# Self-attention's queries and keys projected with features on partitions, two tiles of tokens at a time

## What is computed

```python
x = x + xattn(layernorm(x), ctx_768, mask, Wq, Wk, Wv, Wo)
# self-attention, 16 heads of 32 features
y = layernorm(x)
q = (y @ wq).reshape(b, s, 16, 32)
k = (y @ wk).reshape(b, s, 16, 32)
v = (y @ wv).reshape(b, s, 16, 32)
q, k = rope(q), rope(k)      # out[2i] = t[2i]*cos - t[2i+1]*sin
                             # out[2i+1] = t[2i]*sin + t[2i+1]*cos
p = softmax(where(causal, q @ k.T / sqrt(32), -inf))
x = x + (p @ v) @ wo
x = x + ffn(layernorm(x), ...)
```

## Time and profile before

| | us |
|---|---|
| median of 3 runs (1341.51 to 1342.31) | 1341.54 |
| the profiled execution | 1341.61 |
| its span, first to last instruction | 1339.8 |
| PE busy in the span | 1326.3 |
| POOL busy, 284 instructions | 545.6 |

### The profile page before, as it was taken

The page is one execution under the profiler, slowest core; times in us unless marked ns, Lnnn a source line. Parts: engine busy times, 40 slices in busy tenths (PEclk is TensorE's granted clock), DMA queues, the critical chain, the costliest instruction groups (busy, mean ns, idle before and its releaser), DMA issues.

```text
span 1339.8 us, 33391 instructions
## 1 busy us (share of the span) xinstructions
PE 1326.3 (99%) x13124; PEld 1049.8 (78%) x13124; DVE 689.2 (51%) x1693; ACT 728.6 (54%) x1412; POOL 545.6 (41%) x284
## 2 busy tenths in 40 slices
PE   7999999999999999999999999999999999999998
PEld 6877777777777777777777777778888888888786
DVE  4254544545445444545445444446666578755623
ACT  6455656656566656656566565665343355634231
POOL 6722422432342233224224323654434444473562
PEclk9999999999999999999999999999999999999999
DMA  7101010010001111111100103010000002333241
GB/s 261 60 27 34 29 57 26 33 55 29 33 33 51 33 33 51 33 33 29 55 31 28 59 25 127 14 57 2 2 1 0 0 2 65 95 94 95 79 141 63
DMA packets 39333, 66.20 MB, mean 49 GB/s; under 512 B 4208, under 2 KB 8560, under 8 KB 39280
## 3 DMA queue, kind: packets, MB, share of 16 engines
q1 hardware_dynamic: 38848, 64.67, 14.8%
q10 hardware_dynamic: 432, 0.79, 0.2%
HBM read 61.25 MB, written 4.19 MB: 49 GB/s over the span
## 4 chain that ended last, share of the span: by engine, by line
PE 96%; DVE 1%; POOL 1%; ACT 1%; issue 0%; DMA 0%; POOLq 0%; DVEq 0%
PE psum L205 41%; PE psum L990 9%; PE psum L253 8%; PE psum L1972 7%; PE psum L1596 7%; PE psum L223 5%; PE psum L241 5%; PE psum L1014 3%; PE psum L262 3%; PE psum L775 2%; PE psum L1032 1%; PE psum L1024 1%; PE psum L1042 1%; PE psum L1571 1%; PE psum L1079 0%; PE psum L1074 0%
## 5 line engine op out<-in xcount | busy, mean ns | idle before, releaser
L303 ACT ACTIVATE PT<-psum 128x512 f32<-128x512 f32 x256 | 153.2, 598 | 225.2 <-PE psum L253 225.2
L290 ACT ACTIVATE prob<-prob,nmx 128x512 f32<-128x512 f32 x256 | 182.6, 714 | 96.5 <-DVE nmx L349 96.5
L363 DVE COPY V<-psum 128x512 f32<-128x512 f32 x128 | 88.6, 692 | 228.1 <-PE psum L205 228.1
L349 DVE CUSTOM_DVE_ANT_0 prob<-psum,mbias 128x512 f32<-128x512 f32 x256 | 165.4, 684 | 67.1 <-PE psum L223 67.1
L296 ACT ACTIVATE prob<-prob,rinv 128x512 f32<-128x512 f32 x256 | 182.7, 714 | 0.0
L496 POOL TENSOR_SCALAR ctx_a<-ctx_r 128x1536 fp32r<-128x1536 f32 x16 | 65.4, 4090 | 279.9 <-PE psum L205 279.7
L496 POOL TENSOR_SCALAR ctx_b<-ctx_r 128x1536 fp32r<-128x1536 f32 x16 | 65.4, 4091 | 235.4 <-PE psum L205 235.4
L253 PEld LDWEIGHTS psum<-ident,prob 128*128 128x128 f32 x1024 | 127.6, 141 | 33.4
L253 PE MATMUL psum<-ident,prob 128*128 128x128 f32 x1024 | 153.1, 272 | 0.0
L205 PE MATMUL psum<-wv_h,ctx_b 128*128 128x512 f32 x384 | 144.4, 417 | 0.0
L205 PE MATMUL psum<-wv_h,ctx_a 128*128 128x512 f32 x384 | 142.1, 412 | 0.0
(11 more groups left out here) (236 smaller groups left out, 2810.3 us busy)
## 6 DMA issues: line engine op xcount, KB each, us to landing
ctx_r<-in_ctx SPq DMA_DIRECT2D x32, 768.0 KB, 4.6
w_r<-in_L_ffn_W SPq DMA_DIRECT2D x64, 256.0 KB, 2.8
xres<-in_x SPq DMA_DIRECT2D x16, 256.0 KB, 2.6
out<-tok SPq DMA_DIRECT2D x13, 256.0 KB, 3.0
tok<-in_x SPq DMA_DIRECT2D x3, 1024.0 KB, 11.9
mask<-in_mask_BxS_bf SPq DMA_DIRECT2D x32, 64.0 KB, 4.1
tok<-in_x SPq DMA_DIRECT2D x4, 256.0 KB, 3.4
wq_r<-in_L_xattn_Wq SPq DMA_DIRECT2D x4, 256.0 KB, 5.1
```

What stands on the lines that cost most here:

```text
L290: act.activation(prob[:, r, :], prob[:, r, :], ACT.Exp, bias=nmx[:, r:r + 1], scale=-1.0, accum_out=rsum[:, r:r + 1]).then_inc(s_ex, 1)
L303: act.activation(PT[:, r, :, :].rearrange("p k n -> p (k n)"), T_bank, ACT.Copy).then_inc(s_Pt, 1)
L349: dve.tensor_tensor_reduce(prob[:, r, :], S_bank[r], mbias[:, b, :], 1.0, 3.0e38, ALU.add, ALU.min, nmx[:, r:r + 1]).then_inc(s_mx, 1)
L363: dve.tensor_copy(item_place(q, m), KV_bank[m % 2]).then_inc(s_KVe, 1)
```

## The change

Queries and keys are now computed transposed: the weights are the stationary operand (128 of their columns), and the tokens of a pair of tiles stream past them (256 columns), so the result has features on partitions and needs no transposes. One unit is q or k of one pair: 48 matmuls of 128x256, in four blocks of 12; an even step makes the queries of the pair t+2, t+3, an odd step the keys of that pair. Blocks 0 and 1 go into bank 2, 2 and 3 into bank 3, and each bank is rotated by itself. A rotation is now a product with the cosines and a shuffle of partitions on DVE, a product with the sines and a sum on POOL (`pool_rotate`). ACT's copies of q and k are gone. The tokens of tile t+4 are transposed in step t (before t+2), which takes a second pair of buffers. The loop has four steps in its body. At the end of the cross-attention PE now makes queries and keys of pair 0 and transposes the tokens of tiles 1 to 3, and `v_bank` is gone: values always go into bank 1 behind `s3_od` (tile 15's into bank 3).

```diff
+        def project_pair(pe, b, pair, w_h, w_l, blocks):
+            y_h, y_l = x3_h[pair], x3_l[pair]
+            for j in blocks:
+                out = b[:, j % 2 * 2 * P:(j % 2 + 1) * 2 * P].rearrange("p (t n) -> p t n", t=2)
+                for k in range(DT):
+                    for i, (w, y) in enumerate(((w_h, y_h), (w_l, y_h), (w_h, y_l))):
+                        ins = pe.matmul(out, w[:, k, j * P:(j + 1) * P], y[:, :, k, :], ...)
...
         # pe3
+            if units(t):
+                pe.wait_ge(s3_xl, min(t + 4, G) if isinstance(t, int) else t + 4)
+                pe.wait_ge(s3_rq, 2 * t + 4)
+                at_least(pe, s3_x, t - 2)
+                project_pair(pe, bank[2], pair, w_h, w_l, (0, 1)).then_inc(s3_Q, 1)
+                pe.wait_ge(s3_rk, 2 * t + 4)
+                project_pair(pe, bank[3], pair, w_h, w_l, (2,))
...
-                for n in range(DT):
-                    ins = pe.transpose(bank[0][:, n * P:(n + 1) * P], q_r[:, n * P:(n + 1) * P], ident[:])
...
+            if has(t + 4):
+                pe.wait_ge(s3_rk, 2 * t + 6)
+                pe_x(pe, t + 4, bank[3])
             if has(t + 1) and not (isinstance(t, int) and t == G - 2):
...
+                at_least(pe, s3_od, t)
+                pe.wait_ge(s3_v, t + 1)
+                project_values(pe, bank[1], ph + 1).then_inc(s3_V, 1)
...
+        def rotate(dve, place, rotated):
+            dve.tensor_tensor(by_position(r_cos[:]), by_position(place),
+                              rope[:, 0:1, :].broadcast_to([P, UNIT, SQ]), ALU.mult).then_inc(rotated, 1)
+            dve.stream_shuffle(r_sin[:], place, SWAP).then_inc(rotated, 1)
+        def rotate_low(dve, t):
+            dve.wait_ge(s3_Q, t + 3)
+            at_least(dve, s3_ak, t + 2)
+            rotate(dve, bank[2], s3_rq)
+        def rotate_high(dve, t):
+            dve.wait_ge(s3_K, t + 3)
+            dve.wait_ge(s3_aq, t + 3)
+            rotate(dve, bank[3], s3_rk)
+        def pool_rotate(pool, t, ph, h, rotated, done):
+            x = (k_T if ph % 2 else q_T)[1 - ph // 2]
+            pool.wait_ge(rotated, 2 * t + 6)
+            pool.tensor_tensor(by_position(r_sin[:]), by_position(r_sin[:]),
+                               rope[:, 1:2, :].broadcast_to([P, UNIT, SQ]), ALU.mult).then_inc(s3_am, 1)
+            pool.wait_ge(s3_am, 2 * t + 5 + h)
+            at_least(pool, s3_S, t)
+            pool.tensor_tensor(x[:, 2 * h:2 * h + 2]..., r_cos[:], r_sin[:], ALU.add).then_inc(done, 1)
```

More of the change, by code:

```diff
@@ L900, in dve_cross @@
             END = G - 1, GPT - 1
+            dve_x(dve, 1, 1, bank[2])
             for r in range(3):
@@ L992, in project, with project_values @@
             return ins
[L994 to L1000, removed]
-            return ins
+        def project_pair(pe, b, pair, w_h, w_l, blocks):
[4 more added lines that the diff above has]
+                    for i, (w, y) in enumerate(((w_h, y_h), (w_l, y_h), (w_h, y_l))):
+                        ins = pe.matmul(out, w[:, k, j * P:(j + 1) * P], y[:, :, k, :], start=(k == 0 and i == 0),
+                                        stop=(k == DT - 1 and i == PRODUCTS - 1))
+            return ins
+        def project_values(pe, b, ph):
+            pair, e = ph // 2 % 2, ph % 2
+            return project(pe, b, x3_h[pair][:, e], x3_l[pair][:, e], vw_h, vw_l)
         def pe_x(pe, t, place):
@@ L1016, in output_projection, with scores @@
             return ins
-        def scores(pe):
+        def scores(pe, ph):
+            pair, e = ph // 2 % 2, ph % 2
             for n in range(DT):
@@ L1188, in act3 @@
                 act_normalize(act, 1, (2, 3))
-            if has(t + 2):
-                act_x(act, t + 2, par, x_bank(t + 2))
+            if has(t + 4):
+                act_x(act, t + 4, ph, bank[3])
             if has(t):
@@ L1306, in dve3 @@
                 dve.tensor_tensor(one_tile(t - 2), bank[2], one_tile(t - 2), ALU.add).then_inc(s3_x, 1)
-            if has(t + 2):
-                dve_x(dve, t + 2, par, x_bank(t + 2))
+            if has(t + 4):
+                dve_x(dve, t + 4, ph, bank[3])
             if isinstance(t, int) and t == G - 3:
@@ L1351, in steps @@
             for t in range(4):
-                step(eng, t, t % 2)
-            with eng.Fori(2, G // 2 - 2) as h:
-                for i in range(2):
-                    step(eng, 2 * h + i, i)
+                step(eng, t, t)
+            with eng.Fori(1, G // 4 - 1) as h:
+                for i in range(4):
+                    step(eng, 4 * h + i, i)
             for t in range(G - 4, end):
-                step(eng, t, t % 2)
+                step(eng, t, t % 4)
         KB = 1024
```

289 lines of the change are left out of this document (122 added, 167 removed).

## The result

| | before | after |
|---|---|---|
| median, us | 1341.82 (1341.51 to 1342.31, 4 runs) | 1351.53 (1350.41 to 1353.31, 4 runs) |
| ratio, with its 95% interval | | 1.0073 [1.0056, 1.0091] |
| profiled execution and its span | 1341.61, 1339.8 | 1350.41, 1348.6 |

A forecast was written before the change was run, and what follows sets the result against it. PE, busy 99% of the span, was taken as the bound, with DVE's list nearly as long. Work -12.4, waits +3.8, +13.1 and +7.6, less 1.8 of old gaps, gave +10.3 on 1341.54: 1352 us, range 1338 to 1362.

The forecast's parts named there:

- rival A: Whole kernel: waits outweigh the work saved, so it is slower, 1345 to 1359 us; chance 0.62.
- PE's work, -12.4: On PE: transposes of q and k save 13.9 us, narrower projection matmuls add 1.5; net -12.4 if nothing waits.
- Rival E: PE's projections: pieced moving operand or unhidden weight loads make matmuls dearer, over 1430 us; chance 0.01.
- The rotation: On DVE and POOL: about 1.3 us on DVE, shuffle 0.69, POOL 2.74; one half a serial chain of 4.44.
- Rival D: Rotation chain dearer: POOL's product of 1.91 gives 1362 us, a shuffle of 1.21 gives 1367; chance 0.09.
- The steady wait, 0.38 a step: Steps 3 to 12: PE waits 0.38 us before the values, step 14.84; 3.8 us over ten steps.
- First steps, 13.1: Cross-attention's end and steps 0 to 2: PE waits behind DVE and POOL, 0.8 + 2.0 + 2.3 + 5.1 + 2.9 us.
- The term for the probabilities of step 1: Step 1: PE arrives before step 0's mask-to-probabilities chain through DVE and POOL is done, and waits 2.2 us.
- The term for step 2: Step 2: values wait 2.7 us for DVE's output, tokens 0.2; DVE's split of the output weights holds POOL.
- The end, 7.6: From step 13 on: no projections left to cover the softmax chain and router work; PE waits 7.6 us.
- Old gaps, 1.8: Steps 0 to 2 and the end: about 1.8 us of similar small gaps existed before, so taken off the waits.
- Rival B: Whole kernel faster, PE staying the bound: 1339 us with handovers 0.4 a half shorter, 1329 without waits; chance 0.17.

The follow-up runs named there:

- first_and_last: The change plus a second pair of rotation buffers, with first and last steps reordered: 1337.01 us, 0.9964 of the kernel before.
- filled_gaps: The change, one buffer pair, with unused matmuls in PE's two idle stretches of steps 0 and 1: 1352.21 us, 1.0082 of the kernel before.
- sine_on_vector: The change with the product with the sines moved from POOL to DVE, ahead of the shuffle; POOL then subtracts: 1347.84 us.
- last_steps: The change plus a second pair of rotation buffers, with only the last steps reordered: 1341.19 us.
- first_and_last_2: first_and_last with a looser wait for tokens in odd steps and step 2's whole unit ahead of the probabilities: 1335.23 us, 0.9956 of the kernel before.

## Why the prediction was right

The forecast was 1352, rival A; measured 1351.5. The mechanism was right: the transposes' time is gained, and more than that is lost in waits behind DVE and POOL. That the number is hit within 0.5 us is in part luck, as the sum at the end of this section shows. Point by point:

- **PE's work, -12.4.** Right. Matmuls 0.118 apart, steps of 14.42 with no wait (14.46 forecast). PE's busy time fell 6.0 in the change, but slow-clock stretches are in it; in first_and_last, with the same instructions and no such stretch, it is 1314.6, 11.7 below before. Rival E falls with it, the moving operand's two pieces too. The Trainium skill (TensorE: Matmul & The Clock Gate, The mechanism) says in one place that weight loads overlap running matmuls only where the row group differs, and in another that a load into the background weight buffer is pulled ahead too. The trace fits the second and not the first: loads of 0.188 on the full array lie behind matmuls that start 0.118 apart.
- **The rotation.** DVE 1.24 (r_cos to mask, 994.86 to 996.10) for 1.3; the shuffle 0.735 on average over 32, for 0.69. POOL 1.30 + 0.20 + 1.27 for 2.74. The chain 4.42 for 4.44. Rival D falls. The prediction's estimate of 0.8 for the shuffle, worked out from the Trainium skill (VectorE: DVE Perf Modes, The perf-mode tier table), was a little high.
- **The steady wait, 0.38 a step.** Right in mechanism, which the second buffer pair proves by itself; in size somewhat high. Steps 3 to 12 took 147.94, of which 0.87 is one wait for instructions: 14.71 a step, 0.29 above 14.42.
- **First steps, 13.1.** The waits were 0.23 for 0.8, 1.74 for 2.0, 2.04 for 2.3, 0.26 for 2.2, 2.30 for 2.9, 1.76 for 2.9: 8.3 in all. The term for the probabilities of step 1 was too high since PE came later by the slow stretch, 1.6 us: with the stretches filled that wait was 1.86. The term for step 2 was mis-sized for another reason, for with both stretches filled that wait was still 1.77. There the output projection of tile 0 (2.87 us) stands ahead of the values and covers part of DVE's list, which in step 1 nothing does; the hold of POOL that the term names did come (3.12 for a product of 1.3). 8.3 + 3.2 = 11.5: the clock, which the prediction left out, fills much of the difference. It did less harm than its 3.2 us, because a PE that comes late waits less: of the 3.2, filled_gaps got 1.6 back as a wait.
- **The end, 7.6.** 0.94, 0.43, 0.48, 0.24, 2.17 and 1.41 = 5.7 for 1.9, 0.5, 0.9, 0.7, 2.1 and 1.5. The low part behind the router products was overcharged by 1.0; the product beside POOL is there as forecast (0.72, 1.75 and 1.75 us, before 0.68, 1.76 and 0.68). That the end's waits don't come from the buffers is shown by the same waits with two pairs; that they are lost cover beside DVE's full list is argued, and the new order took 1.7 us of them.
- **Old gaps, 1.8.** PE's only listed wait before in that stretch is 0.7 for instructions, so 1.1 too much was taken off.
- **The signs.** Steps of 14.71 for 14.8 and the MLP 8.8 later for 10, both close to the forecast; an idle of 2 before the probabilities in step 1 did not come (0.26), for the reason above.
- **Rival B** needed handovers 0.4 a half shorter. What brings its case about is another buffer: with it the time is the kernel's before, and with the first and last steps reordered 1335.2, between B's 1329 and 1339.

The measured waits are 8.3 + 2.9 + 0.9 + 5.7 = 17.8, with the clock's 3.2 it is 21.0, less 11.7 of work and 0.7 of an old gap: +8.6, against 8.8 between the spans. The total came out closer than its terms: the waits were forecast 6.7 too long (24.5 for 17.8), and against that stood the clock, which was missing (3.2), work saved that was 0.7 less, and old gaps taken off that were 1.1 less. Of the errors 5.0 cancelled, by luck.

## What to carry to other kernels

Work taken off the bounding engine counts only as far as its neighbours can follow: before removing it, write down the handovers of what replaces it, buffer by buffer, and ask which of them are serial. Here 4 KB of SBUF in each partition for a second pair, on space that the change had itself left free, was worth 9.4 to 9.6 us, nearly all that the change had lost. The steps at either end of a pipelined loop have less cover than the loop; order them anew for the new balance, since there the change waited most: 8.3 us in the first steps (and 3.2 at the lower clock) and 5.7 in the end, against 2.9 in the ten steps between.

## What the runs showed of the hardware

- TensorE's granted clock fell to its lower level behind idle stretches of 1.7 to 2.3 us, in some traced executions and not in others (ahead of the second spread 2.17 and 1.72 us without a fall, 2.18 and 1.72 with one; ahead of the values of tile 2, 2.30 with a fall in the change, 2.30 without in sine_on_vector). What decides it, no run shows. At the lower clock twelve matmuls of 512 columns took about 1.6 us more, a fall lengthened the end by 1.3 to 3.9 us (the table above and the line behind it), and executions of one kernel with a lower mean clock were 2 to 4 us longer (1335.2 and 1339.3, 1346.6 and 1349.2). Gains of 1 us can't be read from one execution.
- A shuffle of partitions of 512 fp32 out of PSUM takes 0.735 us, its mask load 0.01, and the next operation starts 0.62 behind it, the same as behind an elementwise product.
- A small DVE operation on SBUF operands can take much longer beside a POOL operation. In first_and_last the diagonal (256 elements) took 2.00 us beside a POOL subtraction (1125.05 to 1127.23, itself 2.18 for 1.91) that began before it, and 0.42 elsewhere; in last_steps and first_and_last_2, with the same order, it was 2.00 too:

```profile
1125.52 2.00 DVE L1525 TENSOR_TENSOR dg<-fold,s_all 128x256 f32<-128x256 f32 x1
```
